# One attention block of an audio tower: embedding folded into W_k, W_q and W_v, heads by batches on partitions

## What is computed

```python
h = einsum('bnp,dp->bnd', patches, W_tok) + b_tok
x = layernorm(h)
q, k, v = x @ Wq.T, x @ Wk.T, x @ Wv.T
q, k = rope(q, k)
scores = causal(q @ k.T / sqrt(32))
mask = (the key with the largest softmax column sum) | (abs(i - j) <= 1)
attn = softmax(where(mask, scores, lowest)) @ v
h = h + attn @ Wo.T
h = h + (silu(gate(layernorm(h))) * up(layernorm(h))) @ w_down.T
```

## Time and profile before

| | before |
|---|---|
| median of 3 runs | 303.11 us (302.71 to 304.04) |
| the profiled execution: its own time | 301.3 us |
| its span, first to last instruction | 299.5 us |
| busy PE / DVE / ACT / POOL | 276.7 / 162.1 / 80.4 / 84.2 us |
| DMA moved | 39.88 MB |

### The profile page before, as it was taken

The page is one execution under the profiler, slowest core; times in us unless marked ns, Lnnn a source line. Parts: engine busy times, 40 slices in busy tenths (PEclk is TensorE's granted clock), DMA queues, the critical chain, the costliest instruction groups (busy, mean ns, idle before and its releaser), DMA issues.

```text
span 299.5 us, 3612 instructions
## 1 busy us (share of the span) xinstructions
PE 276.7 (92%) x1270; PEld 220.9 (74%) x1270; DVE 162.1 (54%) x293; ACT 80.4 (27%) x133; POOL 84.2 (28%) x61
## 2 busy tenths in 40 slices
PE   2999959994888899999999999999999999999994
PEld 1467828883557677777787567789999999999993
DVE  3657899999679467273810444543343333443323
ACT  4553011004011001145010112334443435434320
POOL 0473696400346410002700000114223222233210
PEclk9999998999999999999999999999999999999999
DMA  7801687574533533435260311548533244330003
GB/s 232 345 0 27 159 266 210 146 247 175 144 103 65 185 126 111 185 118 198 105 206 7 105 42 65 158 148 309 187 112 105 105 130 153 137 105 0 0 0 105
DMA packets 17902, 39.88 MB, mean 133 GB/s; under 512 B 2209, under 2 KB 10657, under 8 KB 17377
## 3 DMA queue, kind: packets, MB, share of 16 engines
q1 hardware_dynamic: 17600, 39.32, 40.6%
q10 hardware_dynamic: 288, 0.39, 0.4%
HBM read 34.46 MB, written 5.24 MB: 133 GB/s over the span
## 4 chain that ended last, share of the span: by engine, by line
PE 72%; issue 11%; DVE 8%; POOL 2%; DMA 2%; SPq 2%; ACT 1%; POOLq 0%; DVEq 0%
PE ps L213 36%; PE ps L995 16%; PE ps L1005 9%; PE ps L963 3%; PE ps L955 3%; DVE prod L241 3%; DMA bias_raw<-b_tok 1%; SPq L278 1%; POOL rot L383 1%; PE ps L899 1%; DVE sm L669 1%; PE ps L924 1%; PE ps L893 1%; POOL prod L245 1%; DVE rot_cos L658 1%
## 5 line engine op out<-in xcount | busy, mean ns | idle before, releaser
L213 PE MATMUL ps<-xT,wgu 128*128 128x384 f32 x384 | 70.9, 340 | 0.1
L213 PEld LDWEIGHTS ps<-xT,wgu 128*128 128x128 f32 x384 | 68.1, 188 | 2.5 <-DVE xT L646 0.9
L995 PE MATMUL ps<-whole,stage 128*128 128x256 f32 (+1 forms) x288 | 58.3, 357 | 1.4 <-ACT whole L451 1.4
L995 PEld LDWEIGHTS ps<-whole,stage 128*128 128x128 f32 x288 | 49.6, 190 | 12.2 <-issue 3.3
L806 DVE TENSOR_TENSOR gu<-silu,ps 128x256 f32<-128x256 f32 (+1 forms) x32 | 15.5, 486 | 78.1 <-PE ps L213 45.2
L362 POOL TENSOR_TENSOR wd<-stage,wd 128x512 fp32r<-128x512 f32 x16 | 26.9, 1682 | 78.6 <-ACT wd L451 78.6
L545 ACT ACTIVATE silu<-ps 128x256 f32<-128x256 f32 (+1 forms) x32 | 14.0, 437 | 83.6 <-PE ps L995 57.2
L213 PE MATMUL ps<-wd,hT 128*128 128x512 f32 x144 | 35.7, 393 | 0.0
L1005 PE MATMUL ps<-stage,gu 128*128 128x512 f32 x64 | 30.1, 593 | 1.5 <-DVE gu L806 1.5
L213 PEld LDWEIGHTS ps<-wd,hT 128*128 128x128 f32 x144 | 26.8, 188 | 5.0
L451 ACT ACTIVATE wgu<-stage 128x1024 fp32r<-128x1024 f32 x16 | 16.9, 1058 | 22.7 <-PE ps L213 20.9
(11 more groups left out here) (81 smaller groups left out, 280.5 us busy)
## 6 DMA issues: line engine op xcount, KB each, us to landing
stage<-w_ffn SPq DMA_DIRECT2D x32, 768.0 KB, 4.3
regroup<-rot SPq DMA_DIRECT2D x40, 64.0 KB, 2.2
regroup<-v_out SPq DMA_DIRECT2D x20, 64.0 KB, 2.3
stage<-w_k SPq DMA_DIRECT2D x1, 1024.0 KB, 6.7
stage<-w_q SPq DMA_DIRECT2D x1, 1024.0 KB, 9.1
stage<-w_v SPq DMA_DIRECT2D x1, 1024.0 KB, 11.1
k_all<-regroup SPq DMA_DIRECT2D x4, 256.0 KB, 2.8
q_all<-regroup SPq DMA_DIRECT2D x4, 256.0 KB, 3.0
```

The costliest lines, as they stand in the source:

```text
L213: ins = pe.matmul(dst, lhs[a], rhs[b], start=first and n == 0, stop=last and n == 2)
L995: ins = pe.matmul(ps[:, bank, at + a:at + b], stage[:, slot, w:w + P], xf[:, k, a:b], start=k == 0, stop=k == KT - 1)
```

## The change

The normalisation is moved behind the projection. LayerNorm subtracts the mean over the 512 columns and divides by the root; the mean can be taken out of W_tok and b_tok once (`average_dims`, then `centred`), and the centred W_tok can be multiplied with W_k, W_q and W_v on the chip (`fold_weight`), which gives a folded matrix of 128 x 512 for each. A projection is then a patch (128 samples) times the folded matrix, plus a folded bias, times the token's inverse root.

`project` now takes 32 batches at one position and one group of 4 heads at a time: the patches are the stationary operand (32 columns), the folded matrix the moving one (128 columns), and the four head groups write to four quarters of the PSUM partitions. So the result already has heads and batches on partitions. One item is up to four positions (PARTS), 16 such products, and two float32r matmuls that add the bias. The products are plain float32. There are 18 items: three parts for each of k, q and v and each group.

The inverse roots reach the same layout through a small matmul (`spread_scale`), and go into the cosine and sine tables (`tables`) and into the copy of v (`drain`, ACT). For group 0 DVE rotates from PSUM as before; for group 1 ACT first copies k and q to SBUF raw, and DVE rotates there in place later (`turn`, now with the addition too). The DRAM buffer, all its transfers, the splits of W_k, W_q, W_v and x, the first normalisation and its transposes are gone; the embedding of h stays, now in plain float32 with the bias product as it was. W_o and the first feed-forward blocks are loaded earlier.

```diff
--- before.py
+++ after.py
...
-PROJECT = [("k", 0), ("q", 0), ("k", 1), ("q", 1), ("k", 2), ("q", 2), ("v", 0), ("v", 1), ("v", 2),
-           ("k", 3), ("q", 3), ("k", 4), ("q", 4), ("v", 3), ("v", 4)]
-ROTATE = [item for item in PROJECT if item[0] != "v"]
-ROT = 4
+PARTS = [(0, 4), (4, 8), (8, 10)]
+PROJECT = [(x, g, n) for g in range(NG) for x in "kqv" for n in range(len(PARTS))]
+ROTATE = [item for item in PROJECT if item[0] != "v" and item[1] == 0]
+DRAIN = [item for item in PROJECT if item not in ROTATE]
+TURN = [(x, n) for n in range(len(PARTS)) for x in "kq"]
...
-            def leave(x, t, buffer, done):
-
-                for q, (g, i) in enumerate(QUADRANTS[t]):
-                    sp.dma_start(regroup["kqv".index(x), g, :, :, i, :].rearrange("h b n -> b h n"),
-                                 buffer[GB * q:GB * (q + 1)].rearrange("p (h n) -> p h n", h=NQ)).then_inc(done, 16)
...
-            def enter(x, t, g, done):
-
-                dst = {"k": k_all, "q": q_all, "v": v_all}[x]
-                own = [i for group, i in QUADRANTS[t] if group == g]
-                at = slice(own[0], own[-1] + 1)
-                sp.dma_start(dst[:, g, at, :], regroup["kqv".index(x), g].rearrange("h b i n -> (h b) i n")[:, at, :])\
-                  .then_inc(done, 16)
...
+            def key_add(n):
...
                 pool.wait_ge(rot_read, n + 1)
...
+                a, b = PARTS[n]
+                pool.tensor_tensor(k_all[:, 0, a:b].rearrange("p i n -> p (i n)"), by_cos[:, n % 2, 0:DH * (b - a)],
+                                   by_sin[:, n % 2, 0:DH * (b - a)], ALU.add).then_inc(key_sum, 1)
+
...
+            def folded(x):
+                act.wait_ge(fold_mm, x + 1)
+                act.activation(fold[:, x], ps[:, FOLD_BANK, :], ACT.Copy).then_inc(fold_sb, 1)
+
+            def folded_bias(x):
+
+                act.wait_ge(fold_bias_mm, x + 1)
+                act.activation(fold_bias[:, x], ps[:, BIAS_BANK, 0:DH], ACT.Copy).then_inc(fold_bias_sb, 1)
+                act.wait_ge(fold_bias_sb, x + 1)
+                split_hi(fold_hi[:, x], fold_bias[:, x], fold_bias_hi)
+
+            def drain(item):
+
+                x, g, n = item
+                a, b = PARTS[n]
+                at = PROJECT.index(item)
+                act.wait_ge(project_mm, at + 1)
+                src = ps[:, PROJECT_BANK[at], :]
+                if x == "v":
+                    act.wait_ge(scale_sb, g + 1)
+                    for i in range(a, b):
+                        last = act.activation(v_all[:, g, i], src[:, DH * (i - a):DH * (i - a + 1)], ACT.Copy, scale=scale[:, g, i:i + 1])
+                else:
+                    dst = {"k": k_all, "q": q_all}[x]
+                    last = act.activation(dst[:, g, a:b].rearrange("p i n -> p (i n)"), src[:, 0:DH * (b - a)], ACT.Copy)
+                last.then_inc(drained, 1)
 
...
+            folded_bias(2)
+            for item in DRAIN[:9]:
+                drain(item)
             exponential(0)
             exponential(1)
             exponential(2)
-            for t in range(NT - 2, NT):
-                values_out(t)
             act.wait_ge(neghalf_set, 1)
             act.activation(warm[:, :], neghalf[:, :], ACT.Silu)
             hi_attn(0)
             hi_attn(1)
+            for item in DRAIN[9:]:
+                drain(item)
             whole_tokens(1)
             whole_tokens(0)
...
+            def token_scale(t):
+
+                inverse_root(t)
+                dve.tensor_scalar(apart[:, t], cut["quad"], rstd[:, t], None, ALU.mult).then_inc(apart_set, 1)
 
...
+            def tables(g):
+
+                dve.wait_ge(scale_mm, g + 1)
+                dve.tensor_copy(scale[:, g], ps[:, SCALE_BANK[g], 0:NPOS]).then_inc(scale_sb, 1)
+                dve.wait_ge(scale_sb, g + 1)
+                for table, angle in ((tcos, "cos"), (tsin, "sin")):
+                    last = dve.tensor_tensor(table[:, g], cut[angle].rearrange("p (i d) -> p i d", d=HD),
+                                             repeated(scale[:, g], 2, HD), ALU.mult)
+                step(last)
+
+            def rotation(src, g, part, buffer):
+
+                a, b = part
+                by = [f[:, buffer, 0:DH * (b - a)] for f in (by_cos, by_sin)]
+                dve.tensor_tensor(by[0].rearrange("p (i h d) -> p i h d", h=HQ, d=HD), src.rearrange("p (i h d) -> p i h d", h=HQ, d=HD),
+                                  repeated(tcos[:, g, a:b], 2, HQ), ALU.mult)
+                halves = [x.rearrange("p (i h a d) -> p i h a d", h=HQ, a=2, d=HD // 2) for x in (by[1], src)]
+                angle = tsin[:, g, a:b].rearrange("p i (a d) -> p i a d", a=2)
+                for n in range(2):
+                    last = dve.tensor_tensor(halves[0][:, :, :, n], halves[1][:, :, :, 1 - n],
+                                             repeated(angle[:, :, n], 2, HQ), ALU.mult)
+                return by, last
+
+            def rotate(x, n):
+
+                m, at = ROTATE.index((x, 0, n)), PROJECT.index((x, 0, n))
+                a, b = PARTS[n]
                 dve.wait_ge(project_mm, at + 1)
-                if n >= 2:
-                    dve.wait_ge(rot_sum, n - 1)
-                src = ps[:, PROJECT_BANK[at % len(PROJECT_BANK)], :].rearrange("p (h a d) -> p h a d", h=H, a=2)
-                cos, sin = (cut[f + x][:, HD * t:HD * (t + 1)].rearrange("p (a d) -> p a d", a=2) for f in ("cos", "sin"))
-                by_cos, by_sin = (f[:, n % 2].rearrange("p (h a d) -> p h a d", h=H, a=2) for f in (rot_cos, rot_sin))
-                dve.tensor_tensor(by_cos, src, repeated(cos, 1, H), ALU.mult)
-                for a in range(2):
-                    last = dve.tensor_tensor(by_sin[:, :, a], src[:, :, 1 - a], repeated(sin[:, a], 1, H), ALU.mult)
+                if m >= 2:
+                    dve.wait_ge(key_sum, min(m - 1, len(PARTS)))
+                if m >= len(PARTS) + 2:
+                    dve.wait_ge(query_sum, m - 1 - len(PARTS))
+                by, last = rotation(ps[:, PROJECT_BANK[at], 0:DH * (b - a)], 0, (a, b), m % 2)
                 last.then_inc(rot_read, 1)
+                if x == "q":
+                    dve.wait_ge(rot_read, m + 1)
+                    dve.tensor_tensor(q_all[:, 0, a:b].rearrange("p i n -> p (i n)"), by[0], by[1], ALU.add).then_inc(query_sum, 1)
+
+            def turn(x, n):
+
+                m = TURN.index((x, n))
+                a, b = PARTS[n]
+                dve.wait_ge(drained, 1 + DRAIN.index((x, 1, n)))
+                if m >= 2:
+                    dve.wait_ge(turned, m - 1)
+                raw = {"k": k_all, "q": q_all}[x][:, 1, a:b].rearrange("p i n -> p (i n)")
+                by, last = rotation(raw, 1, (a, b), m % 2)
+                step(last)
+                dve.tensor_tensor(raw, by[0], by[1], ALU.add).then_inc(turned, 1)
 
...
+            tables(1)
+            turn("k", 0)
             statistics(LN2[1])
             normalise(LN2[1])
-            rotate("k", 4)
+            turn("q", 0)
             statistics(LN2[0])
             normalise(LN2[0])
-            rotate("q", 4)
+            turn("k", 1)
 
             def lo_gu(i, ring, slot):
...
@@ -830,14 +782,17 @@
                 scores(1, i)
             first_pass(0)
             first_pass(1)
+            turn("q", 1)
+            first_pass(2)
             scores(1, 4)
-            first_pass(2)
             scores(1, 5)
             scores(1, 6)
             first_pass(3)
+            turn("k", 2)
+            turn("q", 2)
             scores(1, 7)
+            first_pass(4)
             scores(1, 8)
-            first_pass(4)
             scores(1, 9)
...
+            def fold_weight(x):
+
+                pe.wait_ge(dma_stage[x], 16)
+                for k in range(KT):
+                    ins = pe.matmul(ps[:, FOLD_BANK, :], centred[:, k, 0:P], stage[:, x, D * k:D * (k + 1)], start=k == 0, stop=k == KT - 1)
+                ins.then_inc(fold_mm, 1)
+                if x:
+                    read_out("fold bias", x - 1)
+                for k in range(KT):
+                    for q in range(NQ):
+                        ins = pe.matmul(ps[GB * q:GB * (q + 1), BIAS_BANK, 0:DH], centred[:, k, P:P + BR],
+                                        stage[:, x, D * k + DH * q:D * k + DH * (q + 1)], start=k == 0, stop=k == KT - 1)
+                ins.then_inc(fold_bias_mm, 1)
+
+            def project(item, last):
+
+                x, g, n = item
+                x, (a, b) = "kqv".index(x), PARTS[n]
+                at = PROJECT.index(item)
+                bank = PROJECT_BANK[at]
+                read_out(*last)
+                pe.wait_ge(fold_sb, x + 1)
+                for i in range(a, b):
+                    t, q = slot_of(g, i)
+                    col = P * t + GB * q
+                    for q in range(NQ):
+                        pe.matmul(ps[GB * q:GB * (q + 1), bank, DH * (i - a):DH * (i - a + 1)], pat[:, col:col + GB],
```

(65 more changed lines are left out.)

422 lines of the change are left out of this document (175 added, 247 removed).

## The result

The changed kernel takes **299.99 us** (median of 19 runs, 299.02 to 302.72). The kernel before, run beside it, takes 303.05 (19 runs, 299.95 to 304.04). The ratio is 0.9929, with a 95% interval of 0.9903 to 0.9954: 1.4 to 2.9 us faster. (The medians are of all runs; the ratio leaves disturbed ones out.) I had predicted 311.0, 7.9 us slower. The profiled span went from 299.5 to 297.2.

What follows compares the result with a forecast made beforehand. The start of the first down product was taken to bound the kernel, behind a chain through PE, DVE and ACT. 4.0 + 0.7 + 3.2 = +7.9 us gave 311.0 against the median of 303.11; range 299 to 320, likeliest 305 to 320.

Steps and rivals of the forecast that it cites:

- the term c: PE's time for one product of 32 stationary and 128 moving columns: taken as 0.108 us, between 0.06 and 0.24.
- my floor: Lowest time for one small product on PE: four head groups on four quarters run at once, 0.24 / 4 = 0.06 us.
- Rival 1: Small products on PE overlap fully across the quarters, 0.06 us each: 300.8 us, chance 0.19.
- the signs of being wrong: In the trace: 16 products in 1.0 us or in 3.8; the exponential waiting for DVE; T0 not at about 106.
- The switch: w, PE's cost per change between array shapes: 0.2 us, bounds 0.1 and 0.29; 39 up to group 1's last q.
- PE's other terms: PE's start, embeddings, average and biases to 12.2 us; then folds 10.3, embeddings 3 and 4 2.2, scale 0.15, bias pairs 6.0.
- The wait that decides: ACT's exponential waits for its copies of group 1's k and q, moving `softmax_out(0)` from 62.46 to 66.5: +4.0 us.
- T0: Start of the first down product on PE, 98.2 us before; the change was taken to be worth what it moves this.
- DVE's chain behind q0: DVE's rotation, scores and softmax after q's first item of group 0: 24.3 us, letting `softmax_out(0)` start at 60.1.
- the second formula: T0 moves by end of q's first item minus 34.3, if larger than end of group 1's q minus 57.5.
- The stretch to T0: From `softmax_out(0)` to the first down product: `token_scale(4)` adds 0.7 us, `turn` beside POOL's products and what follows 3.2.
- Later waits do not take it back: After T0 DVE is busy 41.1 of 87 us, so the about 4 us of `turn` it gets there fit.

Runs made afterwards that it cites:

- q_outer: Changed kernel with the loop over quarters outermost in `project`, so four products in a row use the same quarter: 308.65 us (one run).
- product_first: Changed kernel with the first two gate products on DVE ahead of `turn("k", 1)` and the four scores of batch 1: 297.07 us, ratio 0.9794.
- turn_late: Changed kernel with `turn("q", 0)` behind the second norm of tile 0 instead of ahead of it: 301.95 us, ratio 0.9992.
- keep_busy: Changed kernel with PE computing the three v items of group 1 three times, same output: 299.94 us, ratio 0.9938.
- pairs: Changed kernel with two positions of the same quarter in a row in `project`, then the next quarter: 300.95 us, ratio 0.9955.
- all_and_busy: Changed kernel with first gate products, `statistics(4)`, `power(4)` earlier, `turn("q", 0)` behind those products, `token_scale(4)` in DVE's wait, v items computed three times: 295.06 us, ratio 0.9728.

## Why the prediction was wrong, point by point

- **The step that failed is the term c.** I took 0.108 between 0.06 and 0.24, because "the two records of a product need the same quarter one after the other, and records run in order". Measured: 0.055, a little under my floor: the records of four quarters start together, and only those of one quarter follow each other by 0.109. 248 products times 0.053 too much are 13.1 us, and 39 switches at 0.165 for 0.2 are 1.4: 14.5 of the 14.8 by which the end of q, 65.4, missed the 50.6 measured. Rival 1 was what happened. That its time, 300.8, lies so near the 299.99 is in part luck: it had q's first item end at 31.6 for 30.4, and the way from there to `softmax_out(0)` 24.3 long for 25.9, and the two misses cancel. Two of the signs of being wrong that I had named came: 16 products in 1.0 us, and the exponential waiting for DVE.
- **The rule of the Trainium skill.** The row shows 0.24 / 0.055 = 4.4 times the rate of 128-column products with 32 stationary columns four abreast. The Trainium skill (Tensor Engine, "TensorE: Matmul & The Clock Gate", Part 3) states 3.07x for four tiles of rows and 2.38x for three of columns; by it c would be 0.078, an estimate, and the result 303.6. It was nearer than mine, and the measurement is beyond both.
- **The switch.** 0.13 into the shape and 0.20 out of it at 2.4 GHz, inside my bounds. The Trainium skill (TensorEngine Tiling, Key Properties) says that a change of the tiling mode drains the engine. The trace agrees in so far as each change costs this much.
- **PE's other terms held.** The first fold started at 11.97 for my 12.2. With the measured c and w the two sums give 51.0 for the end of q (50.6 measured) and 30.6 for q's first item (30.37).
- **The wait that decides** did not occur here, and it did in `q_outer`, where `softmax_out(0)` started 1.0 after the end of q and T0 came within 0.5 of the formula. The mechanism was right; its condition was not met. In my sums that was an end of q after 59.0; with `softmax_out(0)` at 56.26 as measured it is one after 55.2, and q ended at 50.6.
- **DVE's chain behind q0.** 21.7 predicted from the first rotation to the softmax, 53.63 - 30.41 = 23.2 measured. These 1.5 us are most of the 1.7 by which the second formula misses: it gives 30.37 - 34.3 = -3.9, and T0 moved by -2.2. DVE waited 0.87 and 1.43 for two of POOL's products, where I had charged 0.75 in all.
- **The stretch to T0**: 3.9 predicted (0.7 and 3.2), 3.97 measured. Its parts: 0.69 for `token_scale(4)`; 0.59 more for the value sums, which I had not foreseen (4.53 at a granted clock of 0.50 up to 70 us, where the kernel before took 3.94, from 72.91 to 76.85, at 1.00); 2.29 up to the norm of tile 0 behind `turn("q", 0)` (I had 2.5), with `by_sin` 2.97 long beside POOL; 0.40 behind it. The last was 0.7 in my sum: `turn("k", 1)` took 3.99 (87.75 to 91.74) where I had charged 4.3, and the four scores 3.68 where I had 3.8.
- **"Later waits do not take it back"** held: 201.2 from T0 on, in the changed kernel and in `product_first`; a wait of 0.66 showed only when `turn("q", 0)` too was put there. I had left out the clock, which in `turn_late`, `keep_busy` and `pairs` fell behind the pause at T0 and took 1.6 to 3.1 more.
- **The range** held the result at its edge, with 0.19 on the case that came true; the weights were wrong. Between a floor and a ceiling that lie apart by four, I let one argument about records settle what no row showed, and the argument was about the hardware, not from the trace.

## What to carry to other kernels

Small products that write to different quarters of the output partitions run side by side, also when two in a row share a quarter. For the shape measured here, count them at a quarter of the full product's time, plus 0.13 us for the change into the shape and 0.20 for the change back, and let no more than two in a row share a quarter. When such a change makes a stage short, look at what now stands in the way of the first consumer: here 7.7 us of another engine's work, in the order in which it was written, held it up by 2.9 us, and moving it was worth as much as the change. Judge a change and its best order together, and give the kernel before the same reordering, or the credit goes to the wrong one.

## What the runs showed of the hardware

Four products of 32 stationary and 128 moving columns in float32, on four quarters, take 0.22 us together, as long as one alone (0.24); eight records lie in the time of two. With two of a quarter in a row it is 0.23, with four in a row 0.57.

The granted clock falls behind pauses, and not alike in every execution: after one of 2.90 us at the first down product it stayed at 1.00 in the profile of the changed kernel and fell to 0.50 in that of `keep_busy`, for 1.5 us more on four records. It fell, too, in `all_and_busy`, behind 4 us in which PE was busy for 2.0.

A VectorE operation with both inputs in SBUF that meets GpSimd's product waits for the rest of it: `by_sin` took 2.97 us (80.56 to 83.53, 0.6 after the end of POOL's product) beside POOL's product, whose row is the first below, and 0.75 alone, the second. The sine product of the kernel before, which reads one input from PSUM, did not wait: it took 0.75, the third row, beside POOL's product at 85.04.

```profile
80.12 2.79 POOL L232 TENSOR_TENSOR prod<-v_all,pr 128x1280 f32<-128x1280 f32 x1 [1.29 <-DVE xn L559]
```
```profile
96.68 0.75 DVE L593 TENSOR_TENSOR by_sin<-q_all,tsin 128x256 f32<-128x256 f32 x2
```
```profile
85.47 0.75 DVE L660 TENSOR_TENSOR rot_sin<-ps,const 128x256 f32<-128x256 f32 x2
```
